# Gated cross-attention and expert layer: context laid out transposed in device memory, split into two parts on GpSimd, weights loaded in half-width pieces

## The chip, the cores and the metric

The kernel runs on one core of a Trainium2 chip. The metric is the device time of one execution in microseconds (us), given as the median of several. PE is TensorE, DVE is VectorE, ACT is ScalarE, POOL is GpSimd and SP is SyncE, which issues all DMAs here.

## The reference

For 8 batches of 224 tokens with 512 features, and a context of 750 rows of 512 features per batch:

```python
q = (layernorm(x) @ Wq).reshape(B, N, 8, 64)          # B=8, N=224
k = (ctx @ Wk).reshape(B, M, 8, 64)                   # M=750
v = (ctx @ Wv).reshape(B, M, 8, 64)
attn = softmax(einsum('bihd,bjhd->bhij', q, k) * 64**-0.5)
x = x + tanh(g_xattn) * (einsum('bhij,bjhd->bihd', attn, v).reshape(B, N, 512) @ Wo + bo)
y = layernorm(x)                                      # then 8 experts, 512 -> 1024 -> 512, all summed
h = gelu(einsum('nd,edh->neh', y, w1) + b1)
x = x + tanh(g_ffn) * (norm_gate(y) * (einsum('neh,ehd->ned', h, w2) + b2).sum over experts)
```

## The kernel before

Every float32 product is made of three fast matmuls: an operand is split into a rounded part ("hi", type fp32r) and the rest ("lo"), and `three` (L489) issues hi·hi, hi·lo and lo·hi. For an operand that PE has just put into PSUM, ACT copies hi out of PSUM and DVE subtracts to get lo.

The attention part is software-pipelined over the 8 batches. Work is written as items, and every engine walks the same list of items and does its share of each, so that the list sets the order on all engines. The kinds that matter here are these:

- `C` (before: one of six tiles of 125 context rows): PE transposes `ctx_raw` in four 125x125 transposes, ACT and DVE write hi and lo to `ctxT`.
- `K` and `V`: keys and values out of `ctxT`; `Q`: queries out of `xnT`. Q is drained by four ACT copies and four DVE instructions (L791).
- `L` and `A`: statistics of the layer norm on DVE, with the power -0.5 on POOL (L1119), and its application on DVE (L718). `X`: transposes of the result.
- `S`: scores of one head and half of the queries; a reduce on DVE (L810) and an exponential on ACT (L1000) follow. `R`: the reciprocal of the row sum on DVE (L816). `M`: scaling of the probabilities, one half on ACT, the other on POOL (L1129). `T`: transposes of the probabilities (L569). `P`: probabilities times values (L582). `D`: its result is added up on DVE (L834); after an odd head, POOL splits it into `attT` (L1138, L1140), and after head 3 it also adds the bias to `xres` (L1160).

`HEAD_PLAN` does what must precede batch 0. Then `body_plan` goes through the heads h = 0 to 7 of a batch in the steps `D F0 T0 F1 R0 R1 F2 T1 T2 M0 M1 S0 S1 F3 P`. `FILL[h]` names what is put in at F0 to F3: the second half of this batch's keys and values (db = 0), and those of the next batch (db = 1). `NORMS` hangs `L` and `A` behind other items: `("L",1,0,1)` stands behind `("T",0,4,1)` and `("A",1,0,1)` behind `("T",0,4,2)`. The plan runs once for batch 0, in a loop for batches 1 to 6, and once for batch 7, without the db = 1 items. The items that use PSUM take four banks in turn (`banks`): PE may start one only when the item four places earlier in that ring has been drained. Behind the attention comes a long part for the experts.

Of the kernel before, what the change touches and what calls it, by code (L numbers as in the profile page):

```python
# [11 lines left out]
P = 128  # L39
B, NQ, D = 8, 224, 512  # L40
NK = 750
# [6 lines left out]
CR = 3  # L48
SK = NK // 3
HALVES = [(0, 376), (376, NK)]  # L50
N = B * NQ
# [10 lines left out]
def number(item, b):  # L62
# [5 lines left out]
    if kind == "C":  # L68
        return n * NKT + (item[2] + 1)
    if kind in ("X", "O", "Y"):  # L70
        return n * 2 + (item[2] + 1)
    if kind == "K":
        return n * 8 + (item[2] * 4 + item[3] * 2 + item[4] + 1)
# [6 lines left out]
    if kind in "SRM":  # L80
# [7 lines left out]
BANKED = "CXKQVTOYPB"  # L88
# [15 lines left out]
]  # L104

# [17 lines left out]
def body_plan(first, last):  # L123

    plan = []
    for h in range(H):
# [11 lines left out]
        for item in items:  # L138
            plan += [item] + NORMS.get(item, [])
        if last and h >= G:  # L140
# [8 lines left out]
HEAD_PLAN = [("L", 0, 0, 0), ("L", 0, 0, 1), ("A", 0, 0, 0), ("A", 0, 0, 1), ("C", 0, 0), ("C", 0, 1), ("X", 0, 0),  # L149
# [4 lines left out]

SPLIT_AT = [("X", 0, 0), ("C", 0, 3)]
# [32 lines left out]
def flamingo_kernel(nc, x, ctx, g_xattn, g_ffn, Wq, Wk, Wv, Wo, bo, gate_w, gate_b, rms_w, w1, b1, w2, b2, out,  # L188
# [13 lines left out]
    with ExitStack() as st:  # L202
# [14 lines left out]
        with ExitStack() as att:  # L217
# [14 lines left out]
            ctx_raw = a("ctx_raw", [P, CR, D])  # L232
            xnT = a("xnT", [P, 2, KC, NQ], F32R)
            kst[1] = a("keys1", [P, G, NK], F32R)
# [4 lines left out]
            with ExitStack() as staging:  # L239
                w_raw = alloc(staging, "w_raw", [P, 4, KC, D])  # L240
# [987 lines left out]
```

## Time and profile before

| | |
|---|---|
| median of 3 runs (lowest to highest) | 1986.66 us (1985.81 to 1986.74) |
| profiled execution: span from first to last instruction | 1982.4 us |
| PE busy (matmul) | 1918.0 us, 97% |
| DVE, ACT, POOL busy | 903.9, 780.1, 237.8 us |
| mean granted clock of PE | 0.992 |

The profiled execution has its span, and no device time of its own is recorded for it; the median is 4.3 us above the span. The attention part ends at about 750 us of the span, the experts take the rest. A busy share is an average over these parts, so that the timeline of one batch says more than the table. In a timeline row the bracket at the end is the idle time of the engine ahead of the row and what ended it; a row with x12 holds twelve instructions in succession.

### The profile page before, as it was taken

To read this page: it belongs to the slowest core of one execution; us is meant where nothing else is said; L and a number is where in the kernel's file an instruction comes from. 1 tells how busy PE (TensorE), PEld (TensorE's weight loads), DVE (VectorE), ACT (ScalarE), POOL (GpSimd) and SP (SyncE) were. 2 spreads that over 40 slices of the span, in tenths; PEclk is the share of its full clock that TensorE was granted. 3 is DMA by queue.
4 is the path that set the end of the run, shared out by engine and by line. 5 is a ranking of instruction groups with operands and counts; after the bars stand their busy time and mean duration, and the time that the engine had idled before them with its cause. 6 is when DMAs were issued, how large, how long until landed. Compare 5 with 4: busy or idle time off the path is not lost.

```text
span 1982.4 us, 30405 instructions
## 1 busy us (share of the span) xinstructions
PE 1918.0 (97%) x10933; PEld 1719.5 (87%) x10933; DVE 903.9 (46%) x1621; ACT 780.1 (39%) x1532; POOL 237.8 (12%) x194
## 2 busy tenths in 40 slices
PE   4999999999999988999999999999999999999999
PEld 4999999999999977898898898898898898888888
DVE  3677777777777764233124124124115114214232
ACT  3676766767666641222222232222223213212231
POOL 3223232323323231000000000000000000000000
PEclk9999999999999988999999999999999999999999
DMA  5002021110201052002002002002002002002021
GB/s 160 16 22 74 11 73 32 45 57 21 72 19 48 29 201 93 1 22 64 0 1 84 0 0 85 0 0 85 0 0 77 8 0 74 11 0 70 4 78 61
DMA packets 53836, 84.01 MB, mean 42 GB/s; under 512 B 20192, under 2 KB 22304, under 8 KB 53792
## 3 DMA queue, kind: packets, MB, share of 16 engines
q1 hardware_dynamic: 53792, 83.42, 13.5%
q8 instruction: 28, 0.46, 0.1%
q14 instruction: 16, 0.13, 0.0%
HBM read 68.72 MB, written 14.68 MB: 42 GB/s over the span
## 4 chain that ended last, share of the span: by engine, by line
PE 61%; DVE 1%; issue 0%; ACT 0%; DVEq 0%
PE bank L494 31%; PE scores L494 30%; PE scores L681 0%; DVE w2s L865 0%; DVE w2s L722 0%; DVE hs L722 0%; PE bank L691 0%; DVE x_tile L954 0%; DVE acc L892 0%; ACT hs L1066 0%; DVEq L894 0%; DVEq L891 0%
## 5 line engine op out<-in xcount | busy, mean ns | idle before, releaser
L494 PE MATMUL bank<-w2s,hs 128*128 128x512 f32 x2688 | 619.7, 391 | 4.9 <-DVE w2s L722 2.5
L494 PE MATMUL scores<-xT,w1s 128*128 128x384 f32 (+1 forms) x3072 | 621.2, 362 | 1.0 <-DVE w1s L722 1.0
L494 PEld LDWEIGHTS scores<-xT,w1s 128*128 128x128 f32 x3072 | 555.1, 188 | 62.7 <-DVE w1s L722 1.2
L494 PEld LDWEIGHTS bank<-w2s,hs 128*128 128x128 f32 x2688 | 506.4, 189 | 111.2 <-DVE w2s L722 5.8
L1065 ACT ACTIVATE h_full<-scores,b1T 128x512 f32<-128x512 f32 (+1 forms) x256 | 162.5, 635 | 883.1 <-PE scores L494 876.4
L722 DVE TENSOR_TENSOR hs<-h_full,hs 128x512 fp32r<-128x512 f32 (+1 forms) x256 | 161.3, 630 | 426.5 <-ACT hs L1066 425.7
L892 DVE TENSOR_TENSOR acc<-bank,acc 128x512 f32<-128x512 f32 x112 | 77.4, 691 | 426.1 <-PE bank L494 426.1
L1129 POOL TENSOR_SCALAR probs<-probs,row_inv 112x750 f32<-112x750 f32 x64 | 139.6, 2181 | 249.6 <-DVE row_inv L816 249.6
L1066 ACT ACTIVATE hs<-scores,b1T 128x512 fp32r<-128x512 f32 (+1 forms) x256 | 160.7, 628 | 0.0
L494 PE MATMUL bank<-ctxT,wk 128*128 128x376 f32 (+1 forms) x768 | 147.6, 342 | 8.4 <-DVE ctxT L722 7.5
L494 PE MATMUL bank<-wv,ctxT 128*125 128x256 f32 x1152 | 152.7, 283 | 2.9 <-DVE queries L791 2.9
L1000 ACT ACTIVATE probs<-scores,neg_max 112x750 f32<-112x750 f32 x128 | 112.5, 884 | 97.6 <-DVE neg_max L810 97.6
L494 PEld LDWEIGHTS bank<-wv,ctxT 128*125 128x125 f32 x1152 | 142.9, 186 | 4.9 <-DVE queries L791 4.2
L494 PEld LDWEIGHTS bank<-ctxT,wk 128*128 128x128 f32 x768 | 131.9, 192 | 9.2 <-DVE ctxT L722 7.7
L1189 POOL TENSOR_TENSOR gate_small<-gate_small,minus_half 128x14 f32<-128x14 f32 x1 | 2.6, 2597 | 1104.1 <-DVE gate_small L931 1104.1
L569 PE MATMUL bank<-ident,probs 112*125 112x112 f32 x768 | 110.9, 279 | 13.5 <-DVE keys L722 6.5
L722 DVE TENSOR_TENSOR probsT<-bank,probsT 125x448 fp32r<-125x448 f32 x192 | 114.3, 619 | 7.4 <-ACT probsT L975 5.0
L569 PEld LDWEIGHTS bank<-ident,probs 112*125 112x125 f32 x768 | 99.0, 191 | 20.3 <-DVE keys L722 8.0
L810 DVE TENSOR_REDUCE neg_max<-scores 112x1 f32<-112x750 f32 x128 | 113.8, 929 | 0.4 <-PE scores L559 0.3
L559 PE MATMUL scores<-keys,queries 128*112 128x250 f32 x768 | 106.3, 288 | 3.3 <-DVE queries L791 3.0
L975 ACT ACTIVATE probsT<-bank 125x448 fp32r<-125x448 f32 x192 | 99.1, 545 | 14.9 <-PE bank L569 11.1
L582 PE MATMUL bank<-probsT,values 125*128 125x224 f32 x768 | 98.4, 278 | 1.6 <-DVE probsT L722 1.6
(98 smaller groups left out, 1336.2 us busy)
## 6 DMA issues: line engine op xcount, KB each, us to landing
w_stage<-in_L_ffn_w SPq DMA_DIRECT2D x64, 512.0 KB, 3.5
ctx_raw<-in_ctx SPq DMA_DIRECT2D x48, 250.0 KB
xt_scratch<-yT SPq DMA_DIRECT2D x32, 224.0 KB, 3.1
xT<-xt_scratch SPq DMA_DIRECT2D x4, 1024.0 KB, 9.0
xa<-in_x SPq DMA_DIRECT2D x16, 224.0 KB, 3.8
xres<-in_x SPq DMA_DIRECT2D x16, 224.0 KB, 2.7
x_scratch<-xres SPq DMA_DIRECT2D x16, 224.0 KB, 2.3
x_tile<-x_scratch SPq DMA_DIRECT2D x14, 256.0 KB, 2.6
```

The costliest lines, as they stand in the source:

```text
L494: mm = pe.matmul(bank, s[i], m[j], start=first and n == 0, stop=last and n == total - 1)
L559: last = pe.matmul(ps_scores[qt][0:QT, third, 0:SK], qst[g][:, s, hh, rows], kst[g][:, hh, third * SK:(third + 1) * SK], start=s == 0, sto ...
L569: last = pe.transpose(bank[0:KT, at:at + QT], probs[0:QT, (h % 2) * 2 + qt, kt * KT:(kt + 1) * KT], ident[0:QT, 0:QT])
L582: last = pe.matmul(bank[:, 0:NQ], v, probsT[0:KT, s, kt // 2, (kt % 2) * NQ:(kt % 2 + 1) * NQ], start=kt == 0 and s == 0, stop=kt == NKT - ...
L722: return dve.tensor_tensor(out, a_, b_.bitcast(F32), ALU.subtract)
L810: dve.tensor_reduce(neg_max[0:QT, i:i + 1], ps_scores[qt][0:QT, 0:3, 0:SK], AX.XY, ALU.max, negate=True).then_inc(max_out, 1)
L892: dve.tensor_tensor(acc[:, k, :], ps[k % 2][:, :], acc[:, k, :], ALU.add).then_inc(y_added, 1)
L975: return act.activation(dst, src, ACT.Copy, scale=scale)
L1000: act.activation(probs[0:QT, i, :].rearrange("p (a k) -> p a k", a=3), ps_scores[qt][0:QT, 0:3, 0:SK], ACT.Exp, bias=neg_max[0:QT, i:i + 1 ...
L1065: act.activation(h_full[:, t % 2, 0:nt * P], hb[t % 4][:, 0:nt * P], ACT.Gelu, bias=bias)
L1066: act.activation(hs[:, 0, t, 0:nt * P], hb[t % 4][:, 0:nt * P], ACT.Gelu, bias=bias).then_inc(h_act, 1)
L1129: pool.tensor_scalar(probs[0:QT, i, :], probs[0:QT, i, :], row_inv[0:QT, i:i + 1], None, ALU.mult).then_inc(probs_scaled[qt], 1)
```

## The change

The host hands the context over as (batch, 128, 4, 750), so that it arrives with the feature on the partition and needs no transposing. PE, ACT and DVE no longer have `C` items in a batch. POOL makes both parts instead, out of `ctx_raw`, in two halves of 376 and 374 keys with four chunks each (`CTX_SPLIT`), a copy and a subtraction per chunk. `ctx_raw` now holds one half, so that the second half's load waits for the split of the first. Items `K` for the second pair of heads move in `FILL`; a `V` waits for a whole half. In the head, ACT and DVE split the context, and the weights come in eight pieces of 256 columns (`N` items), five of them split by POOL.

```diff
 FILL = [
-    [[("K", 0, 1, 0, 0), ("Q", 0, 1, 0)], [("K", 0, 1, 0, 1)], [], [("O", -1, 0)]],
-    [[], [], [("K", 0, 1, 1, 0)], [("O", -1, 1), ("V", 0, 1, 0), ("Y", -1, 0), ("K", 0, 1, 1, 1), ("V", 0, 1, 1)]],
+    [[("K", 0, 1, 0, 0), ("Q", 0, 1, 0)], [("K", 0, 1, 1, 0)], [], [("O", -1, 0)]],
+    [[], [], [("K", 0, 1, 0, 1)], [("O", -1, 1), ("V", 0, 1, 0), ("Y", -1, 0), ("K", 0, 1, 1, 1), ("V", 0, 1, 1)]],
     [[], [], [("V", 0, 1, 2)], []],
-    [[("V", 0, 1, 3)], [("V", 0, 1, 4), ("Y", -1, 1), ("C", 1, 0), ("Q", 0, 1, 1)], [("C", 1, 1)], [("V", 0, 1, 5)]],
-    [[], [("V", 1, 0, 0), ("C", 1, 2), ("C", 1, 3), ("C", 1, 4)],
-     [("X", 1, 0)], [("V", 1, 0, 1), ("K", 1, 0, 0, 0), ("V", 1, 0, 2)]],
-    [[("X", 1, 1)], [("C", 1, 5)], [], []],
-    [[("K", 1, 0, 0, 1)], [("Q", 1, 0, 0)], [("K", 1, 0, 1, 0)], [("V", 1, 0, 3), ("K", 1, 0, 1, 1)]],
+    [[("V", 0, 1, 3)], [("V", 0, 1, 4), ("Y", -1, 1), ("Q", 0, 1, 1)], [], [("V", 0, 1, 5)]],
+    [[], [], [("X", 1, 0)], [("V", 1, 0, 0), ("V", 1, 0, 1), ("K", 1, 0, 0, 0), ("V", 1, 0, 2)]],
+    [[("X", 1, 1)], [], [("K", 1, 0, 1, 0)], []],
+    [[("K", 1, 0, 0, 1)], [("Q", 1, 0, 0)], [], [("V", 1, 0, 3), ("K", 1, 0, 1, 1)]],
...
+CTX_SPLIT = {("V", 0, 1, 5): [("C", 1, 0, c) for c in range(KC)],
+             ("V", 1, 0, 2): [("C", 1, 1, c) for c in range(KC)]}
...
+WEIGHT_PIECES = [("wk", 0), ("wq", 0), ("wv", 0), ("wk", 1), ("wq", 1), ("wv", 1), ("wo", 0), ("wo", 1)]
+POOL_PIECES = (2, 4, 5, 6, 7)
+GW = G * DH
+
+HEAD_PLAN = ([("N", 0, 0)] + [("C", 0, 0, c) for c in range(KC)]
+             + [("K", 0, 0, 0, 0), ("L", 0, 0, 0), ("L", 0, 0, 1), ("A", 0, 0, 0), ("A", 0, 0, 1), ("K", 0, 0, 1, 0),
+                ("X", 0, 0), ("X", 0, 1), ("N", 0, 1), ("N", 0, 2)]
+             + [("C", 0, 1, c) for c in range(KC)]
+             + [("Q", 0, 0, 0), ("K", 0, 0, 0, 1), ("K", 0, 0, 1, 1), ("Q", 0, 0, 1), ("S", 0, 0, 0), ("S", 0, 0, 1),
+                ("N", 0, 3), ("N", 0, 4), ("V", 0, 0, 0), ("M", 0, 0, 0), ("M", 0, 0, 1), ("R", 0, 0, 0), ("R", 0, 0, 1),
+                ("V", 0, 0, 1), ("S", 0, 1, 0), ("N", 0, 5), ("V", 0, 0, 2), ("V", 0, 0, 3), ("S", 0, 1, 1),
+                ("V", 0, 0, 4), ("V", 0, 0, 5), ("N", 0, 6), ("N", 0, 7)])
...
+                elif kind == "C" and db:
+                    _, _, half, c = item
+                    k0, k1 = HALVES[half]
+                    if c == 0:
+
+                        pool.wait_ge(in_psum["K"], number(("K", 0, 1, 1, half), b))
+                        pool.wait_ge(in_psum["V"], number(("V", 0, 1, 5 if half else 3), b))
+                        pool.wait_ge(ctx_loaded[half], (b + db) * 16 + 16)
+                    alone(pool, passed["pool"])
+                    pool.tensor_copy(ctxT[:, 0, c, k0:k1], ctx_raw[:, c, 0:k1 - k0]).then_inc(hi_out["C"], 1)
+                    pool.wait_ge(hi_out["C"], number(item, b))
+                    alone(pool, passed["pool"])
+                    pool.tensor_tensor(ctxT[:, 1, c, k0:k1], ctx_raw[:, c, 0:k1 - k0],
+                                       ctxT[:, 0, c, k0:k1].bitcast(F32), ALU.subtract).then_inc(lo_out["C"], 1)
...
-            pe.wait_ge(pool_w_lo, 2)
+            pe.wait_ge(w_lo, 3)
+            pe.wait_ge(pool_w_lo, len(POOL_PIECES))
...
+            a = _np.ascontiguousarray(a.reshape(B, NK, KC, P).transpose(0, 3, 2, 1))
```

The instructions of POOL in the loop over the middle batches, from the scaling of head 4 (in step M1 of head 3) to that of head 5 (in head 4), before:

```order
L1129 TENSOR_SCALAR probs<-probs,row_inv 112x750
L1134 REGISTER_ALU
L1138 CAST attT<-att_sum 128x224
L1139 REGISTER_ALU
L1140 TENSOR_TENSOR attT<-att_sum,attT 128x224
L1159 REGISTER_ALU
L1160 TENSOR_TENSOR xres<-xres,bo_t 112x512 x2
L1119 TENSOR_TENSOR rstd<-rstd,minus_half 112x1
L1127 REGISTER_ALU
L1129 TENSOR_SCALAR probs<-probs,row_inv 112x750
```

The end of the same stretch's new part with the change, that is the last of its four chunks and what follows it at once:

```order
L1158 CAST ctxT<-ctx_raw 128x376
L1159 REGISTER_ALU
L1161 TENSOR_TENSOR ctxT<-ctx_raw,ctxT 128x376
L1119 REGISTER_ALU
L1123 CAST attT<-att_sum 128x224
L1124 REGISTER_ALU
L1125 TENSOR_TENSOR attT<-att_sum,attT 128x224
L1168 REGISTER_ALU
```

Four copies and four subtractions of the context (the rows show one pair) now stand between the scaling and the split of `attT`; behind them follow, as before, the two additions to `xres`, the power for `rstd` and the scaling of head 5.

The instructions of PE in the same loop, from the last keys item ahead of head 6 to the scores of the next batch's head 0, before:

```order
L494 MATMUL bank<-ctxT,wk 128x374 x12
L569 MATMUL bank<-ident,probs 125x112 x4
L494 MATMUL bank<-xnT,wq 128x224 x12
L494 MATMUL bank<-ctxT,wk 128x376 x12
L516 REGISTER_ALU
L569 MATMUL bank<-ident,probs 125x112 x4
```

With the change, where the twelve matmuls of a keys item come in four groups of three and the last group is shown:

```order
L474 MATMUL bank<-ctxT,wk 128x374 x3
L548 MATMUL bank<-ident,probs 125x112 x4
L474 MATMUL bank<-xnT,wq 128x224 x12
L548 MATMUL bank<-ident,probs 125x112 x4
L496 REGISTER_ALU
```

The keys item that stood between the queries (`xnT,wq`) and the transposes of the probabilities has gone to head 5; in both kernels a second group of four transposes and the twelve matmuls of the scores come next.

## Rows read from the trace of the kernel before

**Rows 1.** windows, one steady batch (PE, PEld, DVE, ACT, POOL busy, PEclk, DMA share, GB/s).

```profile
349.00:435.00 86.00, 83.16 (x645) 80.19 (x644) 65.66 (x138) 59.25 (x128) 26.36 (x23) 1.00 0.15 45
```

**Rows 2.** timeline of PE, steady batch (start us, us, engine, line, operation, idle before).

```profile
348.23 0.59 PE L501 MATMUL bank<-ident,ctx_raw 125*128 125x125 f32 x4
348.58 1.58 PE L494 MATMUL bank<-xnT,wq 128*128 128x224 f32 x12
...
358.80 0.65 PE L501 MATMUL bank<-ident,ctx_raw 125*128 125x125 f32 x4 [0.59 <-DVE values L722]
...
371.51 0.69 PE L569 MATMUL bank<-ident,probs 112*125 112x112 f32 x4 [0.93 <-DVE keys L722]
372.04 0.59 PE L501 MATMUL bank<-ident,ctx_raw 125*128 125x125 f32 x4
372.47 1.02 PE L569 MATMUL bank<-ident,probs 112*125 112x112 f32 x8
...
376.06 2.23 PE L494 MATMUL bank<-ctxT,wk 128*128 128x374 f32 x12
...
378.49 1.58 PE L494 MATMUL bank<-xnT,wq 128*128 128x224 f32 x12
...
383.30 1.64 PE L559 MATMUL scores<-keys,queries 128*112 128x250 f32 x12 [0.30 <-DVE queries L791]
...
388.25 1.50 PE L582 MATMUL bank<-probsT,values 125*128 125x224 f32 x12
```

**Rows 3.** timeline of POOL, same batch, from the scaling for head 4.

```profile
353.73 2.17 POOL L1129 TENSOR_SCALAR probs<-probs,row_inv 112x750 f32<-112x750 f32 x1 [4.01 <-DVE row_inv L816]
359.80 0.37 POOL L1138 CAST attT<-att_sum 128x224 fp32r<-128x224 f32 x1 [3.90 <-DVE att_sum L834]
360.26 0.66 POOL L1140 TENSOR_TENSOR attT<-att_sum,attT 128x224 fp32r<-128x224 f32 x1
360.88 2.53 POOL L1160 TENSOR_TENSOR xres<-xres,bo_t 112x512 f32<-112x512 f32 x2
364.75 0.57 POOL L1119 TENSOR_TENSOR rstd<-rstd,minus_half 112x1 f32<-112x1 f32 x1 [1.34 <-DVE rstd L713]
365.31 2.18 POOL L1129 TENSOR_SCALAR probs<-probs,row_inv 112x750 f32<-112x750 f32 x1
```

**Rows 4.** timeline of DVE, same batch.

```profile
353.29 0.22 DVE L816 RECIPROCAL row_inv<-row_sum 112x1 f32<-112x1 f32 x2
...
358.66 0.54 DVE L718 TENSOR_SCALAR xa<-xa,mean_var,rstd 112x512 f32<-112x512 f32 x1
...
365.35 1.12 DVE L718 TENSOR_SCALAR xa<-xa,mean_var,rstd 112x512 f32<-112x512 f32 x1
```

**Rows 5.** timeline of POOL, head plan: weight split and first scaling.

```profile
38.83 1.90 POOL L1168 CAST wo<-w_raw 128x2048 fp32r<-128x2048 f32 x1
40.80 4.58 POOL L1170 TENSOR_TENSOR wo<-w_raw,wo 128x2048 fp32r<-128x2048 f32 x1
53.18 2.18 POOL L1129 TENSOR_SCALAR probs<-probs,row_inv 112x750 f32<-112x750 f32 x1 [7.80 <-DVE row_inv L816]
```

**Rows 6.** timeline of PE, head plan and start of batch 0.

```profile
35.09 4.08 PE L494 MATMUL bank<-ctxT,wk 128*128 128x374 f32 x12 [7.54 <-DVE ctxT L722]
...
40.62 2.23 PE L494 MATMUL bank<-ctxT,wk 128*128 128x376 f32 x12
...
59.86 2.31 PE L494 MATMUL bank<-ctxT,wk 128*128 128x376 f32 x12 [0.87 <-issue]
```

**Rows 7.** windows, start of the program and last batch, columns as Rows 1.

```profile
14.00:16.00 2.00, 0.00 (x0) 0.00 (x0) 1.64 (x7) 0.53 (x1) 0.70 (x2) 1.00 0.33 126
...
700.00:702.00 2.00, 1.09 (x9) 1.09 (x10) 1.45 (x5) 1.95 (x7) 0.46 (x2) 0.95 0.08 13
702.00:704.00 2.00, 2.00 (x11) 2.00 (x11) 2.00 (x6) 1.11 (x2) 2.00 (x3) 0.50 0.31 36
```

More of the change, by code:

```diff
@@ L506, in make @@
                 kind = item[0]
-                if kind in "RMDLAWZ":
+                if kind in "RMDLAWZCN":
                     return
@@ L517, in make @@
                 db = item[1]
-                if kind == "C":
-                    t = item[2]
-                    pe.wait_ge(ctx_loaded[t % CR], (b + db) * (16 * NKT // CR) + 16 * (t // CR + 1))
-                    last = transposes(bank, ctx_raw[:, t % CR, :], KT, P)
-                elif kind == "X":
+                if kind == "X":
                     pe.wait_ge(ln_out, n_ln(0, b + db, item[2]))
@@ L530, in make @@
                     k0, k1 = HALVES[half]
-                    pe.wait_ge(lo_out["C"], number(("C", db, (k1 - 1) // KT), b))
                     cols = slice((2 * g + p) * P, (2 * g + p + 1) * P)
                     keys = slice(k0, k1)
-                    last = three(bank[:, 0:k1 - k0], [([wk[:, s, c, cols] for s in range(2)],
-                                                    [ctxT[:, s, c, keys] for s in range(2)]) for c in range(KC)])
+                    for c in range(KC):
+                        pe.wait_ge(lo_out["C"], number(("C", db, half, c), b))
+                        last = three(bank[:, 0:k1 - k0], [([wk[:, s, c, cols] for s in range(2)],
+                                                           [ctxT[:, s, c, keys] for s in range(2)])],
+                                     first=c == 0, last=c == KC - 1)
                 elif kind == "Q":
@@ L743, in drain @@
                     return
+                if kind == "N":
+                    if item[2] not in POOL_PIECES:
+                        split_w(item[2])
+                    return
+                if kind == "C":
+                    if db == 0:
+                        _, _, half, c = item
+                        k0, k1 = HALVES[half]
+                        dve.wait_ge(hi_out["C"], number(item, b))
+                        sub(ctxT[:, 1, c, k0:k1], (ctx_head if half else ctx_raw)[:, c, 0:k1 - k0],
+                            ctxT[:, 0, c, k0:k1]).then_inc(lo_out["C"], 1)
+                    return
                 if kind == "H":
@@ L768, in drain @@
                 dve.wait_ge(hi_out[kind], n)
[L769 to L774 removed]
+                if kind == "X":
                     cols = slice(item[2] * QT, (item[2] + 1) * QT)
@@ L988, in hi @@
                     return
+                if kind == "N":
+                    name, g = WEIGHT_PIECES[item[2]]
+                    if item[2] not in POOL_PIECES:
+                        w = {"wk": wk, "wq": wq}[name]
+                        act.wait_ge(w_loaded[item[2]], 16)
+                        copy(w[:, 0, :, g * GW:(g + 1) * GW], w_raw[:, item[2]]).then_inc(w_hi, 1)
+                    return
+                if kind == "C":
+                    if db == 0:
+                        _, _, half, c = item
+                        k0, k1 = HALVES[half]
+                        act.wait_ge(ctx_loaded[half], 16)
+                        copy(ctxT[:, 0, c, k0:k1],
+                             (ctx_head if half else ctx_raw)[:, c, 0:k1 - k0]).then_inc(hi_out["C"], 1)
+                    return
                 if kind == "H":
@@ L1014, in hi @@
                 act.wait_ge(in_psum[kind], n)
-                if kind == "C":
-                    t = item[2]
-                    if db:
-                        act.wait_ge(in_psum["K"], number(("K", 0, 1, 1, 1), b))
-                        act.wait_ge(in_psum["V"], number(("V", 0, 1, t), b))
-                    last = copy(ctxT[:, 0, :, t * KT:(t + 1) * KT],
-                                bank[:, 0:KC * KT].rearrange("p (c k) -> p c k", c=KC))
-                elif kind == "X":
+                if kind == "X":
                     if db:
```

133 lines of the change are left out of this document (61 added, 72 removed), and 4 rows, old and new, of the table HEAD_PLAN.

## The prediction

> **What bounds the kernel now.** I read the page first: PE is busy for 97% of the span, so that only PE's own order and its waits can move the time. A change in the attention part counts once per batch, so I then took one steady batch: from 349 to 435 us PE is busy for 83.16 of 86 us at full clock, POOL for only 26.36 [rows 1]. The timeline of PE shows how little is lost: a few gaps below 1 us, which end with a drain by DVE [rows 2]. The timelines of POOL and DVE give the chain that matters for this change: the reciprocal for head 4 at 353.29, POOL's scaling from 353.73 to 355.90, then an idle POOL, the split of `attT`, the bias on `xres`, the power for `rstd` at 364.75, and DVE's second application of the layer norm at 365.35 [rows 3, 4]. The reader is to see that everything in this chain is short, that POOL waits between its members, and that the new work is put exactly there.
>
> **Part 1: what leaves PE.** Six `C` items of four transposes go from each of seven batches (batch 0's leave the head). One costs PE the distance to the next start: 348.58 - 348.23 = 0.35 us, or 372.47 - 372.04 = 0.43 us [rows 2]; six are 2.4 us. The short gaps in front of such items (0.59 at 358.80) and of the transposes of head 5 (0.93 at 371.51) may go as well. That is up to 4 us per batch, if nothing takes their place. ACT's and DVE's shares of `C` lie beside PE's work and are worth nothing by themselves.
>
> **Part 2: what POOL gets.** A chunk is a copy and a subtraction of 128x376. From the rows for 224 and 2048 elements, the copy goes from 0.37 to 1.90 us, so 0.50 for 376; the subtraction goes from 0.66 to 4.58, so 0.99 for 376 [rows 3, 5]. With the 0.09 us from the end of the small copy to the subtraction, a chunk is 1.58 us, a half 6.3 us. Bounds: 4.4 us per half (224-element durations), 8 us if the copies are slowed by half or more beside DVE.
>
> **Part 3: the chain in head 4.** POOL's scaling before it hangs on the queries item at 348.58, whose drains don't change, so that it ends at 355.90 as before, counted from that item. Then:
> - four chunks to 362.3; `attT`, 0.37 + 0.09 + 0.66, to 363.4; `xres`, 2.5, to 365.9; `rstd`, 0.57, to 366.5 [rows 3].
> - DVE's application starts at 366.6 in place of 365.35: 1.25 us later [rows 4]. Behind it on DVE stand the two reduces for the scores, on ACT their exponentials, then the drains of the values and keys items, for which PE's banks wait.
> - In before, PE started head 5's transposes 371.51 - 365.35 = 6.16 us after that application, held by the drain of the keys item [rows 2, 4]. The values item that stood early in head 4 is now drained behind the exponentials too, some 0.4 us more. Head 5 starts at 373.1 in place of 371.5: **1.6 us late**.
>
> PE meanwhile waits in pieces: for the first application (which POOL's copies may slow), for the context at 362.3, and for the bank of `P`. All that ends in the 1.6 us. The second half's chunks (POOL 368.7 to 375) are wanted by PE only near 380; its load of 0.77 MB is issued at 362.3 and is hidden with 6 us to spare.
>
> **Part 4: the moved keys item.** In before, scores start 383.30 - 378.49 = 4.81 us after the start of the queries item on which they depend, with 0.30 us of idle: queries, keys and transposes fill that time [rows 2]. The keys item between them (2.1 us) is now in head 5. The drains of the queries stay, so the distance stays 4.8 us, and PE is idle for 2.4 us of it. Sum: head 6's queries item starts at 373.1 + (378.49 - 371.51) - 0.43 (the `C` item of head 5) + 2.07 (keys item moved ahead) + 0.2 (transposes wait for its drain) = 381.9. Scores start at 386.7 in place of 383.30, **3.4 us late**; from there to `P` of head 6 nothing changes (4.95 us). Less the 0.35 us ahead of 348.58, a batch is 3.05 us longer. Seven batches: +21.4 us.
>
> **Part 5: the clock.** In the last batch PE was busy for 1.09 of 2 us, and in the next 2 us the granted clock is 0.50 (1.2 GHz, where it had been 2.4) [rows 7]. In the head, after a wait of 7.54 us, twelve matmuls took 4.08 us where later ones took 2.23 [rows 6]: 1.9 us lost. The steady batch has no such fall now. It gets waits of 2 to 3 us before head 4's and before head 6's scores and at the `P` of head 4. What falls inside head 4 is mostly hidden by the chain; behind the scores of head 6 nothing hides it. I take 1.6 us a batch (between 0 and 3.5, that is none or two unhidden falls): +11.2 us. The Trainium skill, TensorE: Matmul & The Clock Gate, HAM oscillation, warns of kernels whose short bursts are parted by waits, where the clock is lost again in each round; a clock lost at every one of the waits would take the upper bound here, +24.5 us in place of +11.2. The trace agrees that short gaps are enough in the last batch.
>
> **Part 6: the head.** Context rows are loaded at 126 GB/s with the DMA engines a third busy, since 125 partitions are spread badly [rows 7]; with 128 this should go faster. But batch 0 can't start before POOL has split all its weight pieces. Half a weight costs (1.90 + 4.58)/2 + 0.1 = 3.3 us [rows 5]; three stand behind POOL's first scaling: 2.2 + 10.0 us. That scaling started at 53.18 us. Ahead of it the wait of 7.54 us shrinks, six `C` items at low speed go, and the first weights are smaller: I estimate 12 us earlier (8 to 15). Batch 0 then starts at 41.2 + 12.2 = 53.4 in place of 59.86 [rows 6]: -6.5 us, of which a cold clock after the wait takes 1.7 back. **-4.8 us** (-1 to -9).
>
> **Part 7: POOL and DVE on one port.** The layer norm's application took 0.54 us alone and 1.12 beside POOL's scaling of 2.18 [rows 3, 4]. I keep 1.12 for the second; the first now meets the chunks, +0.6, inside waits that the chain covers. The Trainium skill (SBUF — State Buffer, Who interferes with whom) says that whichever of such a pair starts first holds the shared port for its whole instruction. By that the second application would wait out the 2.18 us of the scaling, +1.1 us per batch in both kernels, and each DVE instruction of this kind that meets a chunk up to 1 us; the row, with both starting together and DVE done after 1.12, doesn't bear that out, and my sum goes by the row.
>
> **Sum.** 21.4 + 11.2 - 4.8 = +27.8 us. The span would be 1982.4 + 27.8 = 2010.2 us, and with the 4.3 us between span and median, the median about 2014.5 us.
>
> **The rivals.**
> - *The waits as summed, the clock holds.* +21.4 - 5 = +16.5: about 2003 us. For it: the steady batch has gaps of 0.9 us and no fall. Against it: the last batch. Chance 0.22.
> - *More than I sum.* POOL's half takes 8 us: another 1.7 us in head 4, or two unhidden falls a batch: 2026 to 2038 us. For it: POOL copies beside DVE. Chance 0.12.
> - *It nets out.* POOL's half takes 4.4 us in place of 6.3, the clock holds, and the head gives its upper bound: head 5 starts 1.9 us earlier than summed, (3.05 - 1.9) x 7 - 9 = -1, about 1986 us. For it: the lower bound of part 2. Against it: both pairs of POOL's rows lie on lines that grow with the elements. Chance 0.08.
> - *Faster.* The queries' drain is what decides. If the scores could start 2.4 us after the queries item rather than 4.8 (because ACT and DVE, without `C`, reach the drain earlier, and PE has nothing between), and head 5 isn't late, then the 2.4 us of transposes and some 1.5 us of gaps come off each batch: 7 x 3.9 + 5 = 32 us, about 1954 us. It decides from 3.4 us between queries and scores on. Against it: ACT's four copies and DVE's four instructions follow each other there and don't wait for `C`. Half of it would still be 1970. Chance 0.10.
>
> My forecast has the remaining 0.48, with a range of its own of 2006 to 2024 us. To leave out no more than 2 in 10, the range takes in the clock that holds and part of the dearer case: 1992 to 2032 us. A difference within 0.2% (4 us) can't be told from none here. Faster by more than that: 0.11, from the last rival and a little of the third; the same: 0.06; slower: 0.83.
>
> **What would show it.** In the timeline of POOL, chunks of about 0.50 and 0.99 us right after the scaling, and `rstd` near 16.5 us after the start of the queries item. In DVE's, an idle time of some 3 us before the second application, ended by POOL. In PE's, about 2.4 us of idle before the scores in head 6, ended by DVE's queries; a steady batch of 88 to 91 us in place of 86; windows at 0.50 of the clock in every batch. Batch 0 should start at about 53 us, PE waiting for POOL. The forecast is wrong if POOL's chunks are much shorter than the rows for 224 and 2048 elements say, if DVE doesn't stand at the second application, or if the head gains more than 15 us.

## The result, and the profile after

| | before | after |
|---|---|---|
| median (lowest to highest) | 1986.52 us (1985.81 to 1986.74), 4 runs | 2010.56 us (2006.96 to 2024.95), 4 runs |
| ratio, with its 95% interval | | 1.0137 (1.0104 to 1.017) |
| profiled execution: span; its device time | 1982.4 us; not recorded | 2008.6 us; 2010.4 us |
| mean granted clock of PE | 0.992 | 0.975 |

The changed kernel is 1.4% slower. PE still sets the time. The windows show that a batch now takes 89.3 us, that PE is busy for 83.34 of them, as long as it was in 86 us before [rows 1], and that the granted clock is no longer 1.00 all through but falls to 0.50 (1.2 GHz) in places. The 24 transposes are gone from these 83.34 us, but the rows at half clock are longer: the same items take 80.65 us where the clock stays at 1.00 (experiment 7). The columns are those of [rows 1]; behind the batch stand pieces of its head 4, of head 6, and of head 6 two batches later.

```profile
357.00:446.30 89.30, 83.34 (x619) 80.34 (x618) 62.85 (x131) 56.16 (x120) 37.24 (x38) 0.96 0.15 43
364.00:366.00 2.00, 0.86 (x6) 0.53 (x5) 1.13 (x2) 1.68 (x4) 1.81 (x3) 1.00 0.00 0
366.00:368.00 2.00, 0.00 (x0) 0.00 (x0) 1.52 (x2) 1.33 (x5) 1.82 (x4) 0.73 0.00 0
368.00:370.00 2.00, 1.95 (x10) 1.95 (x11) 1.48 (x5) 0.61 (x2) 1.77 (x3) 0.50 0.00 0
...
394.00:396.00 2.00, 0.56 (x5) 0.56 (x6) 1.90 (x7) 1.06 (x3) 0.23 (x1) 1.00 0.00 0
...
576.00:578.00 2.00, 2.00 (x11) 2.00 (x11) 1.14 (x2) 1.55 (x3) 0.60 (x1) 0.50 0.00 0
```

The timeline of PE for the same batch, which answers to [rows 2]; the queries item at 357.32 answers to the one at 348.58:

```profile
357.32 1.58 PE L474 MATMUL bank<-xnT,wq 128*128 128x224 f32 x12
...
368.05 1.01 PE L481 MATMUL bank<-ident,xa 112*128 112x112 f32 x4 [2.61 <-DVE xa L699]
368.85 1.89 PE L548 MATMUL bank<-ident,probs 112*125 112x112 f32 x8
370.42 2.82 PE L538 MATMUL scores<-keys,queries 128*112 128x250 f32 x12
373.04 3.32 PE L474 MATMUL bank<-wv,ctxT 128*125 128x256 f32 x24
...
379.70 1.60 PE L561 MATMUL bank<-probsT,values 125*128 125x224 f32 x12
...
381.53 0.66 PE L548 MATMUL bank<-ident,probs 112*125 112x112 f32 x4
...
390.63 1.58 PE L474 MATMUL bank<-xnT,wq 128*128 128x224 f32 x12
...
392.90 0.69 PE L548 MATMUL bank<-ident,probs 112*125 112x112 f32 x4 [0.26 <-DVE keys L703]
395.44 1.64 PE L538 MATMUL scores<-keys,queries 128*112 128x250 f32 x12 [1.85 <-DVE queries L779]
```

Two places differ. In head 4 PE waits 2.61 us for the first layer norm application, and then four transposes take 1.01 us and twelve score matmuls 2.82 us, which take 0.6 and 1.63 at full clock. In head 6 it waits 1.85 us for the queries. The timelines of POOL and DVE, which answer to [rows 3, 4], show the chain in head 4:

```profile
362.46 2.17 POOL L1114 TENSOR_SCALAR probs<-probs,row_inv 112x750 f32<-112x750 f32 x1 [3.59 <-DVE row_inv L804]
364.59 0.50 POOL L1158 CAST ctxT<-ctx_raw 128x376 fp32r<-128x376 f32 x1
365.27 0.98 POOL L1161 TENSOR_TENSOR ctxT<-ctx_raw,ctxT 128x376 fp32r<-128x376 f32 x1 [0.19 <-POOL ctxT L1158]
...
370.93 0.36 POOL L1123 CAST attT<-att_sum 128x224 fp32r<-128x224 f32 x1
371.38 0.66 POOL L1125 TENSOR_TENSOR attT<-att_sum,attT 128x224 fp32r<-128x224 f32 x1
372.00 2.51 POOL L1169 TENSOR_TENSOR xres<-xres,bo_t 112x512 f32<-112x512 f32 x2
374.48 0.56 POOL L1104 TENSOR_TENSOR rstd<-rstd,minus_half 112x1 f32<-112x1 f32 x1
```

```profile
366.81 1.18 DVE L699 TENSOR_SCALAR xa<-xa,mean_var,rstd 112x512 f32<-112x512 f32 x1
...
375.07 1.12 DVE L699 TENSOR_SCALAR xa<-xa,mean_var,rstd 112x512 f32<-112x512 f32 x1 [2.25 <-POOL rstd L1104]
```

`rstd` comes 17.16 us after the start of the queries item, 16.17 before, and DVE stands for 2.25 us at the second application. The head, which answers to [rows 5, 6], in the timelines of POOL and of PE:

```profile
41.89 2.18 POOL L1114 TENSOR_SCALAR probs<-probs,row_inv 112x750 f32<-112x750 f32 x1 [16.42 <-DVE row_inv L804]
...
52.16 2.34 POOL L1147 TENSOR_TENSOR wo<-w_raw,wo 128x1024 fp32r<-128x1024 f32 x1
```

```profile
54.59 4.10 PE L474 MATMUL bank<-ctxT,wk 128*128 128x376 f32 x12 [9.02 <-POOL wo L1147]
```

Where the 26.2 us of span come from can be counted from the start of the queries item in head 3, once in batch 0 and once in the last batch. Seven batches lie between the two. The starts, read from PE's timeline of each kernel:

```
                                    first     last   distance   per batch
before                              91.35   691.27     599.9      85.7
after                               88.05   715.55     627.5      89.6
keys item back                      91.42   698.00     606.6      86.7
keys item forward, in before        91.62   716.64     625.0      89.3
first half in head 3                89.42   695.93     606.5      86.6
first half in head 3, keys back     88.79   672.74     584.0      83.4
first half in head 3, value not     90.66   714.73     624.1      89.2
statistics earlier                  89.64   723.09     633.5      90.5
small chunks on POOL                89.69   709.88     620.2      88.6
```

The batches lose 27.6 us, the head gives back 3.3 (91.35 to 88.05), and what follows the last queries item loses 1.9 more. Each line is one profiled execution. The other six kernels with the changed kernel's head reach the first start at 88.79 to 91.42. In all six ACT waits 3.44 to 4.41 us for the load of the first context half, in the changed kernel's trace only 1.46. So the 3.3 us are the best case of this head, and a difference of up to 3 us between the first starts of two such lines is not the edit's.

### The profile page after: what moved, and what is told of

It is laid out like the page before. It is cut to its first block, busy times and chain, and to the rows that moved or that the text cites. A ratio compares the mean times of both kernels' runs of the same rounds, so it can differ in the third digit from the quotient of the medians.

```text
span 2008.6 us, 29994 instructions
## 1 busy us (share of the span) xinstructions
PE 1921.5 (96%) x10741; PEld 1724.5 (86%) x10741; DVE 889.5 (44%) x1582; ACT 759.3 (38%) x1493; POOL 318.1 (16%) x312
## 4 chain that ended last, share of the span: by engine, by line
PE 60%; DVE 1%; issue 0%; ACT 0%; DVEq 0%
PE bank L474 30%; PE scores L474 30%; PE scores L657 0%; DVE hs L703 0%; DVE w2s L703 0%; DVE w2s L848 0%; PE bank L667 0%; DVE x_tile L937 0%; DVE acc L875 0%; ACT hs L1056 0%; DVEq L877 0%; DVEq L874 0%
## 5 line engine op out<-in xcount | busy, mean ns | idle before, releaser
L474 PE MATMUL bank<-ctxT,wk 128*128 128x376 f32 (+1 forms) x768 | 150.0, 346 | 17.4 <-POOL wo L1147 9.0
L474 PEld LDWEIGHTS bank<-ctxT,wk 128*128 128x128 f32 x768 | 134.3, 196 | 17.6 <-issue 17.5
L474 PEld LDWEIGHTS bank<-wv,ctxT 128*125 128x125 f32 x1152 | 147.3, 192 | 0.8
L548 PE MATMUL bank<-ident,probs 112*125 112x112 f32 x768 | 117.4, 290 | 12.8 <-POOL probs L1114 7.1
L538 PE MATMUL scores<-keys,queries 128*112 128x250 f32 x768 | 114.9, 303 | 14.0 <-DVE queries L779 11.2
L548 PEld LDWEIGHTS bank<-ident,probs 112*125 112x125 f32 x768 | 105.3, 202 | 19.4 <-issue 8.7
L538 PEld LDWEIGHTS scores<-keys,queries 128*112 128x112 f32 x768 | 102.2, 193 | 15.4 <-issue 15.4
L561 PE MATMUL bank<-probsT,values 125*128 125x224 f32 x768 | 103.3, 282 | 4.2 <-DVE probsT L703 3.0
```

Source lines behind the costliest of these rows:

```text
L474: mm = pe.matmul(bank, s[i], m[j], start=first and n == 0, stop=last and n == total - 1)
L538: last = pe.matmul(ps_scores[qt][0:QT, third, 0:SK], qst[g][:, s, hh, rows], kst[g][:, hh, third * SK:(third + 1) * SK], start=s == 0, sto ...
L548: last = pe.transpose(bank[0:KT, at:at + QT], probs[0:QT, (h % 2) * 2 + qt, kt * KT:(kt + 1) * KT], ident[0:QT, 0:QT])
L561: last = pe.matmul(bank[:, 0:NQ], v, probsT[0:KT, s, kt // 2, (kt % 2) * NQ:(kt % 2 + 1) * NQ], start=kt == 0 and s == 0, stop=kt == NKT - ...
```

## The experiments

**1. Keys item back.** Head 6 gets its keys item between queries and scores again; all else is the changed kernel. (The order of the semaphore counts for `K` follows the list.)

```diff
-    [[("X", 1, 1)], [], [("K", 1, 0, 1, 0)], []],
-    [[("K", 1, 0, 0, 1)], [("Q", 1, 0, 0)], [], [("V", 1, 0, 3), ("K", 1, 0, 1, 1)]],
+    [[("X", 1, 1)], [], [], []],
+    [[("K", 1, 0, 0, 1)], [("Q", 1, 0, 0)], [("K", 1, 0, 1, 0)], [("V", 1, 0, 3), ("K", 1, 0, 1, 1)]],
```

> Changed kernel, with the keys item of the second pair put back between the queries and the scores of head 6 (as before the change). Waits theory (the loss of a batch is two waits, scores behind the queries' drain in head 6 and the layer norm behind POOL in head 4): the wait of 1.85 us ahead of the scores goes, and with it the clock falls behind it, so a batch of 89.3 us becomes 87.3 and the whole about 1995 us (1992 to 1999), 15 below the changed kernel. POOL-load rival (what costs is POOL's work and its port, wherever the items stand): no change beyond 3 us, 2008 to 2013. Clock rival (falls of the clock cost most, and this wait is not their cause): 2005 to 2012, with as many windows at 0.50 as now.

Measured: 1989.2 us (11 runs; before 1985.8), ratio 1.0018 (1.0009 to 1.0027). That is 21 us less than the changed kernel, from one item's place, where 15 was expected. In PE's timeline the scores have only a short wait, and no clock fall behind them in any of the seven batches:

```profile
387.06 1.65 PE L540 MATMUL scores<-keys,queries 128*112 128x250 f32 x12 [0.31 <-DVE queries L781]
```

They start 4.81 us after their queries item (382.25), just as in the changed kernel (390.63 to 395.44). The distance is fixed by the drains. What counts is whether 2 us of work lie inside it.

**2. The same move in the kernel before.** No GpSimd split, nothing of the change but the keys item's place.

```diff
-    [[("X", 1, 1)], [("C", 1, 5)], [], []],
-    [[("K", 1, 0, 0, 1)], [("Q", 1, 0, 0)], [("K", 1, 0, 1, 0)], [("V", 1, 0, 3), ("K", 1, 0, 1, 1)]],
+    [[("X", 1, 1)], [("C", 1, 5)], [("K", 1, 0, 1, 0)], []],
+    [[("K", 1, 0, 0, 1)], [("Q", 1, 0, 0)], [], [("V", 1, 0, 3), ("K", 1, 0, 1, 1)]],
```

> The kernel BEFORE with one edit: the next batch's first keys item K(1,0,1,0) goes from between the query projection and the scores of head 6 to head 5, which is where the change has it (in before's own numbering of the K items). Nothing of the context's path is touched. Waits theory: what cost 21 us in the changed kernel (1989.2 with the item back, 2010.6 without) is that nothing stands any more between queries and scores of head 6, so that the scores wait for the split of the queries (idle 1.85 us there in the changed kernel's trace), and it must cost the same here: 7 batches by 1.9 to 2.8 us, +13 to +20, so 1999 to 2007. Rival, load on GpSimd: the keys item's move is only dear beside GpSimd's chunks (which take the queries' split longer); here it costs under 3 us, 1984 to 1990.

Measured: 2007.8 us (4 runs; before 1984.6), ratio 1.0113 (1.0096 to 1.013). So +23 us without any work on POOL: the rival is out, and the waits theory's range was a little short. PE's timeline shows why. The wait is the expected one, and in a later batch the clock falls behind it:

```profile
396.68 1.64 PE L561 MATMUL scores<-keys,queries 128*112 128x250 f32 x12 [1.85 <-DVE queries L793]
398.15 1.58 PE L496 MATMUL bank<-wv,ctxT 128*125 128x256 f32 x12
...
573.40 2.84 PE L561 MATMUL scores<-keys,queries 128*112 128x250 f32 x12 [1.85 <-DVE queries L793]
576.04 2.76 PE L496 MATMUL bank<-wv,ctxT 128*125 128x256 f32 x12
```

The twelve score matmuls and the twelve of the values item run from 573.40 to 578.80 there, 5.4 us; in the rows above it is 3.05. This happens in four of the seven batches. Undisturbed batches are 88.36 us apart, 2.6 more than in before.

**3. Statistics earlier.** The second tile's statistics move ahead of the probabilities' scaling, so that `rstd` is made before the chunks.

```diff
-    ("T", 0, 4, 1): [("L", 1, 0, 1)],
+    ("M", 0, 4, 1): [("L", 1, 0, 1)],
```

> Changed kernel, with the statistics of the second half of x (and POOL's power for rstd) ahead of the context chunks instead of behind them; nothing else moves. Waits theory: DVE's 2.25 us of idle ahead of the second application goes, head 5 starts 1 to 2 us earlier, a batch becomes 87.3 to 88.3 us, and the whole 1996 to 2003 us. POOL-load rival: the same POOL work beside the same DVE work gives 2008 to 2013 us.

Measured: 2013.4 us (4 runs), ratio 1.0139 (1.0123 to 1.0154), no gain. The second application no longer waits for POOL. But the statistics, with a wait of 0.28 us for the load of `xa`, now stand on DVE ahead of the two reduces that precede the first application. In the batch shown it starts 11.02 us after the queries item, where it was 9.49. PE's wait for it grows from 2.61 to 3.56 us (3.28 to 4.40 in the seven batches), and the half clock behind it stays, as its timeline shows.

```profile
373.69 1.01 PE L481 MATMUL bank<-ident,xa 112*128 112x112 f32 x4 [3.56 <-DVE xa L699]
```

Head 5 starts 24.7 us after the queries item, 24.2 in the changed kernel. So the edit opens one path and lengthens another, PE's own through the first application and a cold clock, and by itself it doesn't tell the two apart; its time is near the one that the rival had named (2008 to 2013), which experiment 4 puts out. The changed kernel's own batches show that PE's path is not the only bound either: in one batch the clock still held for the first rows behind the wait (four transposes in 0.60 us at 546.68), and PE simply waited 0.94 us later on for DVE's values. Head 6 began 33.33 us after the queries item there, and 33.31 in the batch shown above. The two bounds end at nearly the same time, so that taking away one gives little while the other stands; experiment 6 shows the other side of it.

**4. Small chunks on POOL.** Each chunk splits only 8 columns; the rest of the context stays that of batch 0, so later batches compute with the wrong context.

```diff
-                    pool.tensor_copy(ctxT[:, 0, c, k0:k1], ctx_raw[:, c, 0:k1 - k0]).then_inc(hi_out["C"], 1)
+                    pool.tensor_copy(ctxT[:, 0, c, k0:k0 + 8], ctx_raw[:, c, 0:8]).then_inc(hi_out["C"], 1)
...
-                    pool.tensor_tensor(ctxT[:, 1, c, k0:k1], ctx_raw[:, c, 0:k1 - k0],
+                    pool.tensor_tensor(ctxT[:, 1, c, k0:k0 + 8], ctx_raw[:, c, 0:8],
```

> Changed kernel, where each of POOL's copies and subtractions of the context in a batch does 8 columns instead of 376; the other columns of the context stay those of the first batch. Instructions and order are the same, POOL's 13 us of chunks per batch become 2. Waits theory: only head 4's wait goes (1 to 2 us a batch), the scores of head 6 still wait for the queries: 1996 to 2003 us. POOL-load rival: all of the loss goes, 1975 to 1987 us.

Measured: 2002.2 us (4 runs), ratio 1.0082 (1.0067 to 1.0098). The four chunks of a half now take POOL 2.1 us instead of 6.4, and only 8 of the 24 us come back, so POOL's load as such is not what the change costs. The time is inside the range of the waits theory and far from the rival's. The batches show where the 8 us lie. The first application, which met the chunks in the changed kernel and took DVE 1.18 us, takes 0.54, and head 6's queries come 0.6 us earlier in each batch, 4.3 in seven. And the clock fell behind head 6's scores in none of them, where it fell in two of the changed kernel, 1.5 us each. DVE's timeline has the application:

```profile
364.98 0.54 DVE L699 TENSOR_SCALAR xa<-xa,mean_var,rstd 112x512 f32<-112x512 f32 x1
```

What remains is in the order of PE's items: the wait for the queries is 1.84 to 1.87 us as before, and this one in head 4 is left in PE's timeline, with the half clock behind it:

```profile
365.57 1.01 PE L481 MATMUL bank<-ident,xa 112*128 112x112 f32 x4 [1.97 <-DVE xa L699]
```

**5. First half in head 3.** The chunks of the first half come ahead of the scaling for head 4, in a stretch in which POOL had been idle for 3.59 us, and the values item V(1,0,0) returns to where it stood in before, ahead of the first tile's transposes.

```diff
-CTX_SPLIT = {("V", 0, 1, 5): [("C", 1, 0, c) for c in range(KC)],
+CTX_SPLIT = {("V", 0, 1, 3): [("C", 1, 0, c) for c in range(KC)],
...
-    [[], [], [("X", 1, 0)], [("V", 1, 0, 0), ("V", 1, 0, 1), ("K", 1, 0, 0, 0), ("V", 1, 0, 2)]],
+    [[], [("V", 1, 0, 0)], [("X", 1, 0)], [("V", 1, 0, 1), ("K", 1, 0, 0, 0), ("V", 1, 0, 2)]],
```

> The changed kernel with the chunks of the first context half placed behind V(0,1,3) (head 3, ahead of the scaling of head 4's scores) and not behind V(0,1,5), and V(1,0,0) put back to head 4's second filler place, where before had it. Keys item stays where the change has it. GpSimd does the same work as in the changed kernel, only earlier, in a stretch in which it idles 3.6 us. Waits theory: rstd no longer comes behind 6.4 us of chunks, so that the second application (idle 2.25) and TensorE's wait for the first (2.61) and the half clock behind it go; V(1,0,0) covers some of what is left. Period 89.3 less 4 to 6.5, total 1965 to 1983. Rival, load on GpSimd (its work on the shared port slows VectorE wherever it runs): the same work moves its harm to head 3, 2000 to 2012.

Measured: 1990.1 us (9 runs; before 1984.6), ratio 1.0027 (1.0017 to 1.0037). 20 us of the 24 come back, 27 to 45 were expected: the waits theory overshot, the load theory missed the other way. PE's timeline shows 0.53 us left of head 4's wait and no half clock behind it, and in this batch a clock fall behind head 6's wait, which is untouched:

```profile
359.14 0.60 PE L481 MATMUL bank<-ident,xa 112*128 112x112 f32 x4 [0.53 <-DVE xa L699]
359.58 1.33 PE L548 MATMUL bank<-ident,probs 112*125 112x112 f32 x8
360.68 1.64 PE L538 MATMUL scores<-keys,queries 128*112 128x250 f32 x12
...
383.99 2.10 PE L538 MATMUL scores<-keys,queries 128*112 128x250 f32 x12 [1.87 <-DVE queries L779]
385.89 2.68 PE L474 MATMUL bank<-wv,ctxT 128*125 128x256 f32 x12
```

The clock falls there in three of seven batches, in two in the changed kernel. A batch without the fall is 86.1 us.

**6. Chunks' move alone.** As 5, but the values item stays behind the transposes (only the first pair of lines of that diff).

> The changed kernel with the chunks of the first context half behind V(0,1,3), and nothing else: V(1,0,0) stays behind the transposes of the first normalised tile, where the change put it (with both edits: 1990.1). Theory by now, value item's place: what cost time in head 4 was that no work stands ahead of that tile's transposes any more (wait of 2.61 us, half clock behind it: 1.0, 1.9 and 2.8 us for rows that take 0.6, 1.3 and 1.65), and the chunks' late place cost because it forbade the item there. Then the chunks' move alone gives little: the wait is still 2.0 to 2.6 and the clock still falls, period 88 to 89.5, total 2000 to 2012. Rival, rstd behind the chunks: the move alone frees the second application, and all of the gain of 20 us is here, 1987 to 1993.

Measured: 2007.7 us (4 runs; before 1985.3), ratio 1.0108 (1.009 to 1.0127). The rival is out: of the 20 us, moving the chunks gives 3 by itself (four runs of 2002.7 to 2010.1, against 2007.0 to 2025.0 of the changed kernel, so that the size of these 3 is uncertain). The values item's return, which that move permits, gives the other 17.6. In PE's timeline the wait has shrunk by 0.65 us only, and clock falls come in head 4 and, in five of the seven batches, behind head 6's queries as well. The last two rows are from a later batch, in which the clock held behind the same wait:

```profile
369.38 0.89 PE L481 MATMUL bank<-ident,xa 112*128 112x112 f32 x4 [1.96 <-DVE xa L699]
...
371.62 2.23 PE L538 MATMUL scores<-keys,queries 128*112 128x250 f32 x12
...
395.56 1.84 PE L538 MATMUL scores<-keys,queries 128*112 128x250 f32 x12 [1.87 <-DVE queries L779]
...
637.45 0.60 PE L481 MATMUL bank<-ident,xa 112*128 112x112 f32 x4 [1.96 <-DVE xa L699]
...
638.70 1.64 PE L538 MATMUL scores<-keys,queries 128*112 128x250 f32 x12
```

In the changed kernel head 5 starts 24.1 to 24.3 us after the queries item in every batch, in experiment 5 after 21.0. Here it depends on the clock: 23.5 to 23.8 in four batches, 22.4 in two in which the clock is back sooner (one is shown first), and 21.3 in the one in which it held. So with POOL's chain out of the way the half clock in head 4 costs up to 2.4 us, and what the values item gives there is above all that the clock doesn't fall; the wait itself is worth 0.3. Up to head 6's queries the chunks' move gains 9.0 us over the seven batches, and the clock behind head 6's scores takes 5.5 back. Why it falls there more often than in the changed kernel was not separated.

**7. Both edits.** Experiments 1 and 5 in one kernel.

> The two edits together on the changed kernel: chunks of the first half behind V(0,1,3) with V(1,0,0) in head 4's second filler place, and the keys item back between queries and scores of head 6. Waits theory: both waits that the change brought in are gone and the 36 transposes with them, period 82 to 84 against 85.77 in before, 1953 to 1970. If only the keys item mattered (its edit alone gave 1989.2): 1986 to 1992.

Measured: 1964.8 us (4 runs; before 1984.6), ratio 0.9902 (0.9885 to 0.9918), a kernel 1% faster than before. (The transposes gone are 24 per batch, not the 36 that the expectation names.) In PE's timeline the same stretch has only short waits:

```profile
349.27 0.60 PE L483 MATMUL bank<-ident,xa 112*128 112x112 f32 x4 [0.54 <-DVE xa L701]
...
360.15 1.58 PE L550 MATMUL bank<-ident,probs 112*125 112x112 f32 x12 [0.93 <-DVE keys L705]
...
371.53 1.65 PE L540 MATMUL scores<-keys,queries 128*112 128x250 f32 x12 [0.31 <-DVE queries L781]
```

The last two are the waits that before had at the same places, 0.93 and 0.30 [rows 2]. The window of one batch, with POOL as busy as in the changed kernel (37.14 us against 37.24) and the clock at 1.00:

```profile
339.20:422.70 83.50, 80.65 (x619) 77.57 (x618) 61.88 (x131) 55.91 (x121) 37.14 (x39) 1.00 0.16 46
```

**8. Head: weights first.** GpSimd's three late weight pieces go ahead of its first scaling.

```diff
-                ("N", 0, 3), ("N", 0, 4), ("V", 0, 0, 0), ("M", 0, 0, 0), ("M", 0, 0, 1), ("R", 0, 0, 0), ("R", 0, 0, 1),
-                ("V", 0, 0, 1), ("S", 0, 1, 0), ("N", 0, 5), ("V", 0, 0, 2), ("V", 0, 0, 3), ("S", 0, 1, 1),
-                ("V", 0, 0, 4), ("V", 0, 0, 5), ("N", 0, 6), ("N", 0, 7)])
+                ("N", 0, 3), ("N", 0, 4), ("N", 0, 5), ("N", 0, 6), ("N", 0, 7), ("V", 0, 0, 0), ("M", 0, 0, 0), ("M", 0, 0, 1), ("R", 0, 0, 0), ("R", 0, 0, 1),
+                ("V", 0, 0, 1), ("S", 0, 1, 0), ("V", 0, 0, 2), ("V", 0, 0, 3), ("S", 0, 1, 1),
+                ("V", 0, 0, 4), ("V", 0, 0, 5)])
```

> Changed kernel, where POOL splits its last three weight pieces before the first scaling of probabilities instead of behind it (they have landed long before, and POOL idles for 16.4 us ahead of that scaling). Waits theory: PE's wait of 9.0 us ahead of batch 0 goes and the cold clock behind it (1.9 us): 1999 to 2002 us, batch 0 starts at 45 to 47 us. Rival (batch 0 is held by something else that is ready at the same time): 2006 to 2011 us.

Measured: 2011.6 us (4 runs), ratio 1.0142 (1.0125 to 1.016), by the edge of the rival's range and far from the 1999 to 2002 of the waits theory. PE's wait ahead of batch 0 fell from 9.02 to 3.57 us, but batch 0 started at 54.45 as against 54.59. The head's scores had slipped from 32.88 to 38.19, 4.5 us of it counted from PE's first queries item (9.63 us after it, and now 14.10), since the pieces met VectorE's four subtractions for the second context half. The timeline of DVE has them in one row, here and in the changed kernel:

```profile
23.96 7.96 DVE L703 TENSOR_TENSOR ctxT<-ctx_head,ctxT 128x374 fp32r<-128x374 f32 x4
```

```profile
7.66 1.93 DVE L703 TENSOR_TENSOR ctxT<-ctx_raw,ctxT 128x376 fp32r<-128x376 f32 x4 [0.67 <-ACT ctxT L958]
...
23.12 4.13 DVE L703 TENSOR_TENSOR ctxT<-ctx_head,ctxT 128x374 fp32r<-128x374 f32 x4
```

**9. The same, one wait more.** POOL starts the first of those pieces only when the context's subtractions are done.

```diff
+                    if item[2] == 5:
+                        pool.wait_ge(lo_out["C"], 2 * KC)
```

> The changed kernel's head with GpSimd's three late weight pieces (5, 6, 7) ahead of its first scaling, as in the run that gave nothing (2011.6), and with one wait more: GpSimd starts piece 5 only when VectorE has done its 12 subtractions of the context. Batches unchanged. If the earlier miss came from the two engines meeting (four of VectorE's subtractions took 7.96 us beside GpSimd's pieces, 1.93 alone), TensorE starts batch 0 at 49 to 51.5 us against 54.6, total 2005 to 2008. Rival, that the head is bound by its own chain of work and not by the pieces: 2010 to 2013, batch 0 at 53.5 or later.

Measured: 2006.1 us (4 runs; before 1984.6), ratio 1.0108 (1.0091 to 1.0125). Adding a wait to the kernel of experiment 8 made it 5.5 us faster, and 4.5 faster than the changed kernel. (The wait is for the eight subtractions of the context, not the 12 that the expectation names.) DVE's row is back at 4.11 us, and PE's timeline has batch 0 at 51.34, which is 25.9 us after PE's first queries item, where it was 31.3 in the changed kernel and 30.4 in experiment 8:

```profile
51.34 3.80 PE L474 MATMUL bank<-ctxT,wk 128*128 128x376 f32 x12 [3.56 <-DVE values L703]
```

**10. All of it.** Experiments 7 and 9 in one kernel.

> The changed kernel with all edits that gave something: first half's chunks behind V(0,1,3), V(1,0,0) back in head 4's second filler place, the keys item back between queries and scores of head 6 (1964.8 so far), and in the head the three late weight pieces ahead of the first scaling, behind VectorE's context subtractions (2006.1 against 2010.6 by itself). If the gains add: 1964.8 less 4.5, so 1958.5 to 1962. If the head's gain is lost in a batch that starts in another phase: 1963 to 1966.

Measured: 1959.3 us (4 runs; before 1985.3), ratio 0.9866 (0.985 to 0.9882). The gains add. This is the best version found, 26 us below before and 51 below the changed kernel.

## Why the prediction was right, and where its terms were off

The kernel is slower by 24 us; 28 were predicted by the sum, and the reason is the one given: two moves in the order of items open waits on PE that cost more than the transposes give. By the prediction's steps:

- **Transposes removed (part 1).** Predicted 2.4 us per batch. With both waits closed (experiment 7) seven batches take 584.0 us against 599.9, that is 2.3 each. The gain is real; the change hid it.
- **POOL's chunks (part 2).** Predicted 0.50 and 0.99 us and 6.3 per half; the rows show 0.50 and 0.98 or 0.85 (one copy of 0.69), and 6.39. Neither bound, 4.4 or 8, was near. With that *It nets out* falls, and the first half of *More than I sum*; its other half, two unhidden clock falls a batch, was two in seven batches.
- **The chain in head 4 (part 3).** The application was predicted at 18.0 us after the queries item and came at 17.75; head 5 was to be 1.6 us late and was 1.3 (24.21 against 22.93). The size was right, but the step named one bound where there are two. The prediction put PE's waits down as something that ends inside the chain, with no cost of their own. PE's wait for the first application, with the half clock behind it, is a path of the same length (experiments 3, 4 and 6). It exists because V(1,0,0) no longer stands ahead of those transposes (experiments 5 and 6). The sign "`rstd` near 16.5 us" did not fit the prediction's own chain, in which it starts at 365.9, 17.4 us after the queries item; it was measured at 17.16.
- **The keys item (part 4).** Queries to scores 4.81 us and scores to `P` 4.95, both as predicted. From head 5 to head 6's queries it was 9.10 us, 8.82 predicted. Of the wait, 2.4 us were predicted, and 1.85 plus 0.26 found. Experiments 1 and 2 show that this item's place costs 21 to 25 us with and without POOL's chunks.
- **The first application beside the chunks (part 7).** Predicted +0.6 us, measured 1.18 against 0.54. That the chain covers it holds only while the chain is there: it is the 0.6 us by which PE's own path gets shorter in experiments 4 and 6.
- **From `P` to the next batch.** 0.35 us less per batch was predicted; it was 0.12 more. Among the new short waits there is one in PE's timeline that the step did not have:

```profile
412.60 1.59 PE L474 MATMUL bank<-xnT,wq 128*128 128x224 f32 x12 [0.28 <-DVE att_sum L822]
```

- **The clock (part 5): the term that was mis-sized.** Predicted 11.2 us, found 3.0 in the profiled execution. The clock does fall in head 4 in every steady batch, which costs nothing in this kernel, since the chain is as long (experiment 6 shows up to 2.4 us where it isn't). Behind head 6's wait, where nothing hides it, it fell in two of seven batches, each 1.5 us longer (90.84 and 90.83 us against 89.3). The Trainium skill's section on HAM oscillation (TensorE: Matmul & The Clock Gate) describes a clock lost again in each round of a kernel with waits. The traces show that in head 4, and at head 6 only in part: with an equal wait of 1.84 to 1.87 us it held in five batches and fell in two here, and fell in none of seven in experiment 4, three in experiment 5, four in experiments 2 and 3, and five in experiment 6. I found no row that tells beforehand which. The runs of the changed kernel differ with their mean clock (2006.96 us at 0.978, 2024.95 at 0.967); that these are more falls of this kind is likely, but only one of the runs has a trace.
- **The sum over batches.** Predicted 32.6 us, 27.6 measured: 8.2 too much for the clock, against 3.2 too little in the rest (3.5 us per undisturbed batch, not 3.05).
- **The head (part 6).** Predicted -4.8, measured -3.3. POOL's scaling came at 41.89 (41.2 predicted), batch 0 at 54.59 (53.4), and the cold clock behind the wait cost 2.3 us in the first keys and queries items (1.7). The loads ran at 326 GB/s from 2 to 8 us and at 353 from 10 to 16, well above the 126 of [rows 7]. Other executions of the same head gain less, down to nothing (91.42 in experiment 1).
- **Not in the sum.** The part behind the last queries item is 1.9 us longer; the mean clock over 30 us of it is 0.72 (730 to 760), 0.83 before (706 to 736). This part takes 1288.1 to 1293.3 us in the twelve traces, so 1.9 is within what one execution differs from another. And the prediction took 4.3 us from the span to the median, where the changed kernel's profiled execution has 1.8 (2010.4 and 2008.6): the 4.3 set the span of one execution against the median of others. Its span, 2010.2 by the prediction's sum, was 2008.6.
- **How near the number came.** The time is 4 us below the 2014.5 of the sum, but the terms were off by more: 8.2 too much for the clock and 2.5 too much from span to median, against 3.2 too little in the batches' waits, 1.5 in the head and 1.9 behind the last queries item. That these cancel so well is luck.

Of the rivals, the clock that holds (2003 us) was nearest behind the forecast: that case describes five batches of seven. The faster one failed where it said it would be decided: 4.81 us from queries to scores, not 3.4.

## What to carry to other kernels

Work that is taken off the bottleneck engine is only worth its time if the order around it still covers the drains that others do. Here the transposes that were removed were worth 16 us, while two other items that had filled the bottleneck's waits were moved along with them and cost 18 us (the values item, experiments 5 and 6) and 21 us (the keys item, experiment 1); putting those two back, and the new work where its engine was idle, turned 1.4% slower into 1.0% faster, and a better order in the head made that 1.3%. Part of what such an item gives is the clock: a wait of 2 us cost 0.3 us by itself and up to 2.4 by the half clock behind it. For each item that is moved, ask what waited behind it in its old place. And when removing a wait gives nothing, look for a second path of the same length before dropping the idea.

## What the runs showed of the hardware that was not expected

A subtraction on DVE with both inputs in SBUF can stand still behind POOL for the rest of POOL's instruction. In the changed kernel's head DVE's four subtractions start at 23.12, while POOL works on `wq`. POOL's timeline:

```profile
22.19 3.27 POOL L1147 TENSOR_TENSOR wq<-w_raw,wq 128x1024 fp32r<-128x1024 f32 x1
```

The trace by tile gives the shortest, the median and the longest of the four in ns:

```profile
L703 DVE TENSOR_TENSOR ctxT<-ctx_head,ctxT x4: 534/534/2753, 23.1 to 26.7; 128x374 fp32r<-128x374 f32 x4
```

One took 2.75 us, until 25.87, and the others 0.53. In experiment 8, where POOL's pieces follow each other, all four were hit:

```profile
L703 DVE TENSOR_TENSOR ctxT<-ctx_head,ctxT x4: 1374/2038/2747, 24.0 to 30.5; 128x374 fp32r<-128x374 f32 x4
```

The Trainium skill (SBUF — State Buffer, Who interferes with whom) says that a DVE instruction with two SBUF inputs contends with a GpSimd instruction that reads SBUF; it says of DVE's modes that use both of its port pairs that whichever instruction issues first keeps the shared pair for its whole length. These rows agree with the first, and the first subtraction's end, 0.4 us after POOL's at 25.46, looks like the same lock, though the page does not count this kind of subtraction among those modes. The prediction had set the rule aside because of the layer norm's application, which took 1.12 us beside a scaling of 2.18; that row stays as it is (1.12 again, 375.07 to 376.19 beside 375.03 to 377.20). So the lock was seen for the subtraction of two tensors and not for the application, and a row of one kind of instruction should not have been read as the answer for the other. In the batches the lock itself can have cost little: DVE's subtractions there have one input in PSUM (`bank`), and the one of `values` took 0.42 us beside POOL's chunks (366.47) too. What did cost time there is the slower application, 1.18 us beside the chunks and 0.54 without them (experiments 4 and 6): 0.6 us per batch.
